# Delta attention: the products of probabilities and values cut into four quarters of TensorE's array

## The reference

```python
def step(carry, seg):
    mem, z = carry
    qq, kk, vv = seg
    sigma_q = jax.nn.elu(qq) + 1.0
    scores = jnp.einsum('bhsk,bhtk->bhst', qq, kk) / scale
    scores = jnp.where(causal_mask, scores, -jnp.inf)
    att_dot = jax.nn.softmax(scores, axis=-1) @ vv
    att_mem = sigma_q @ mem / (sigma_q @ z)
    sigma_k = jax.nn.elu(kk) + 1.0
    delta = vv - sigma_k @ mem / (sigma_k @ z)
    mem_new = mem + jnp.einsum('bhsk,bhsv->bhkv', sigma_k, delta)
    z_new = z + sigma_k.sum(axis=-2, keepdims=True).transpose(0, 1, 3, 2)
    att = beta * att_mem + (1.0 - beta) * att_dot
    out = att.reshape(Bsz, SEG, H * DV) @ Wo
    return (mem_new, z_new), out
```

## Time and profile before

| | us |
|---|---|
| median of 3 runs | 681.11 (678.39 to 682.96) |
| the profiled execution's own time | 681.31 |
| its span in the trace | 679.3 |
| attention, first scores to the last stage's end | about 37 to 425 |

### The profile page before, as it was taken

The page is one execution under the profiler, slowest core; times in us unless marked ns, Lnnn a source line. Parts: engine busy times, 40 slices in busy tenths (PEclk is TensorE's granted clock), DMA queues, the critical chain, the costliest instruction groups (busy, mean ns, idle before and its releaser), DMA issues. The chain is left out here.

```text
span 679.3 us, 12696 instructions
## 1 busy us (share of the span) xinstructions
PE 620.1 (91%) x4390; PEld 523.8 (77%) x4390; DVE 407.5 (60%) x1057; ACT 375.2 (55%) x882; POOL 172.2 (25%) x189
## 2 busy tenths in 40 slices
PE   3999999999999999999999998697999958996796
PEld 3878888988988988988988988586455546985553
DVE  6757595196396196396196273768445479535554
ACT  2679769479569479569469464222466521201242
POOL 4702011011011011011011021342477514301454
PEclk9999999999999999999999999899999978998799
DMA  8200200000120000100000051298233261008631
GB/s 265 78 2 1 81 14 1 3 6 2 34 68 1 2 6 1 32 6 0 5 5 1 3 123 40 73 408 314 62 95 101 73 238 69 0 1 307 235 91 35
DMA packets 25459, 48.99 MB, mean 72 GB/s; under 512 B 4062, under 2 KB 15296, under 8 KB 25408
## 3 DMA queue, kind: packets, MB, share of 16 engines
q1 hardware_dynamic: 19456, 35.74, 15.2%
q0 software_dynamic: 3840, 10.49, 5.1%
q10 hardware_dynamic: 2112, 2.10, 0.9%
HBM read 40.06 MB, written 8.78 MB: 72 GB/s over the span
## 5 line engine op out<-in xcount | busy, mean ns | idle before, releaser
L932 DVE RECIPROCAL denominators<-readings 128x2 f32<-128x2 f32 x128 | 21.3, 167 | 143.8 <-PE readings L572 143.4
L572 PEld LDWEIGHTS readings<-memory_copy,sigma 128*128 128x128 f32 x512 | 75.3, 191 | 11.7 <-ACT memory_copy L779 2.6
L788 ACT ACTIVATE memory_reading<-readings,denominators 64x128 f32<-64x128 f32 x256 | 78.5, 356 | 5.3 <-DVE denominators L932 3.3
L572 PE MATMUL readings<-memory_copy,sigma 128*128 128x129 f32 x512 | 78.7, 275 | 2.6 <-ACT memory_copy L779 2.5
L779 ACT ACTIVATE memory_copy<-memory 128x258 f32<-128x258 f32 x128 | 50.1, 392 | 55.4 <-PE memory L582 40.9
L938 DVE SCALAR_TENSOR_TENSOR minus_delta<-readings,denominators,v 64x128 f32<-64x128 f32 x240 | 73.8, 347 | 4.5 <-DVE denominators L932 0.3
L582 PE MATMUL memory<-minus_delta,sigma_k_tokens 128*128 128x129 f32 x480 | 73.2, 275 | 0.0
L481 POOL TENSOR_TENSOR xn<-scores,exp_sum_inverse 64x512 f32<-64x512 f32 x32 | 33.8, 1055 | 133.8 <-DVE exp_sum_inverse L959 132.6
L472 POOL TENSOR_TENSOR scores<-scores,score_max 128x512 f32<-128x512 f32 x16 | 16.7, 1044 | 195.3 <-DVE score_max L953 195.3
L621 PE MATMUL ahead<-wo,attT 128*128 128x256 f32 x256 | 64.5, 396 | 1.0 <-DVE attT L967 1.0
L582 PEld LDWEIGHTS memory<-minus_delta,sigma_k_tokens 128*128 128x128 f32 x480 | 63.0, 191 | 0.0
(11 more groups left out here) (303 smaller groups left out, 1465.1 us busy)
## 6 DMA issues: line engine op xcount, KB each, us to landing
weights_e<-experts SPq DMA_DIRECT2D x24, 608.0 KB, 12.5
xn<-L_attn_Wq SPq DMA_DIRECT2D x4, 512.0 KB, 4.0
wo<-L_attn_Wo SPq DMA_DIRECT2D x1, 2048.0 KB, 12.9
rows_e<-xn ACTq DMA_DIRECT2D x4, 512.0 KB, 10.8
carried<-L_attn_Wk SPq DMA_DIRECT2D x3, 512.0 KB, 4.8
xn<-L_attn_Wv SPq DMA_DIRECT2D x3, 512.0 KB, 4.0
x<-L_attn_x SPq DMA_DIRECT2D x4, 256.0 KB, 3.5
x<-L_attn_x SPq DMA_DIRECT2D x2, 512.0 KB, 3.5
```

Source lines behind the costliest of these rows:

```text
L572: last = pe.matmul(KQ[g][:, hh * MC:(hh + 1) * MC], sqk[:, GROUP * g + hh, pair, 2 * par:2 * par + 2, :], mz[g][:, hh, :], start=True, sto ...
L788: last = act.activation(read[rows, half, GROUP * g + hh, pair, :], KQ[g][rows, hh * MC:hh * MC + DK], ACT.Copy, scale=nr[g][rows, hh:hh + 1])
```

## The change

Each local product is cut into four matmuls of 64 keys, 64 columns and 64 queries, so that the zero blocks of the probabilities are not multiplied. The two segments of a tile take the two row halves of the array (`par`), and the two halves of a head's 128 columns the two column halves (`c`). A row half writes its own bank, `L[par]`, which now holds both heads. So one burst has 32 matmuls in place of 8, and ScalarE picks each head out of two banks with two instructions of 256 columns. The burst has one semaphore step where it had two. Its waits for `pTs` stand ahead of a full-size matmul: in slot 10 of `project` 10, in slot 14 of `project_out`, and the burst itself comes behind these; where a slot has neither, a transpose of the identity is put in for it (`busy`). Waits for ScalarE's scaling (`bt_copied`) become waits for both heads.

```diff
-                def local(n, half, pp, hh):
-
-                    h = GROUP * pp + hh
-                    pe.wait_ge(pTs_ready, 4 * n + h + 1)
-                    for t in range(TPH):
-                        last = pe.matmul(L[hh][:, t * P:(t + 1) * P], v[:, half * TPH + t, h * DK:(h + 1) * DK],
-                                         pTs[hh][:, t * P:(t + 1) * P], start=True, stop=True)
+                def local(n, half, pp):
+
+                    for hh in range(GROUP):
+                        for t in range(TPH):
+                            for par in range(2):
+                                keys = slice(par * SEG, (par + 1) * SEG)
+                                queries = pTs[hh][keys, t * P + par * SEG:t * P + (par + 1) * SEG]
+                                at = (hh * TPH + t) * SEG
+                                for c in range(2):
+                                    begin = (GROUP * pp + hh) * DK + c * SEG
+                                    last = pe.matmul(L[par][c * SEG:(c + 1) * SEG, at:at + SEG],
+                                                     v[keys, half * TPH + t, begin:begin + SEG], queries,
+                                                     start=True, stop=True)
                     last.then_inc(bt_ready, 1)
...
                     if m == 0:
                         if behind:
-                            pe.wait_ge(bt_copied, 4 * n - 1)
+                            pe.wait_ge(bt_copied, 4 * n)
                         scores(n, half, 0)
...
                     if m == 12:
                         pe.wait_ge(p_ready, 4 * n + 4)
+                        pe.wait_ge(bt_copied, 4 * n + 2)
                         for hh in range(2):
-                            pe.wait_ge(bt_copied, 4 * n + hh + 1)
                             turn_probs(n, 1, hh)
-                    if m in (10, 14):
-                        for hh in range(2):
-                            local(n, half, (m - 10) // 4, hh)
+                    out_at = OUT_AT if ahead else LAST_OUT_AT
+                    if m in (10, 14) and not (ahead if m == 10 else behind and m in out_at):
+                        pe.wait_ge(pTs_ready, 4 * n + (m - 6) // 2)
+                        busy(pe, L[0], ident, 1)
                     if ahead:
                         for what, u in AHEAD_AT.get(m, ()):
+                            if m == 10 and what == "project":
+                                pe.wait_ge(pTs_ready, 4 * n + 2)
                             if what == "turn":
                                 turn_sigma_k(n + 1, 1 - half, u)
                                 continue
...
                             project(n + 1, it + half, 1 - half, u, free)
-                    out_at = OUT_AT if ahead else LAST_OUT_AT
+                    if m == 10:
+                        local(n, half, 0)
+                    if m == 14 and behind and m in out_at:
+                        pe.wait_ge(pTs_ready, 4 * n + 4)
                     if behind and m in out_at:
...
                         project_out(1 - half, out_at[m])
+                    if m == 14:
+                        local(n, half, 1)
...
                 def scale_local(n, half, pp):
 
+                    act.wait_ge(bt_ready, 2 * n + pp + 1)
                     for hh in range(2):
                         h = GROUP * pp + hh
-                        act.wait_ge(bt_ready, 4 * n + h + 1)
-                        act.activation(att[:, half, h, :], L[hh][:, :], ACT.Copy, scale=one_less_q[:, h:h + 1])\
-                           .then_inc(bt_copied, 1)
+                        by_parity = att[:, half, h, :].rearrange("p (t a c) -> p t a c", a=2, c=SEG)
+                        for par in range(2):
+                            src = L[par][:, hh * TPH * SEG:(hh + 1) * TPH * SEG].rearrange("p (t c) -> p t c", c=SEG)
+                            last = act.activation(by_parity[:, :, par, :], src, ACT.Copy, scale=one_less_q[:, h:h + 1])
+                        last.then_inc(bt_copied, 1)
```

More of the change, by code:

```diff
@@ L425, in _ @@
                 next_tiles.load_first(sp, carried)
-                sp.wait_ge(bt_ready, 4 * STAGES)
+                sp.wait_ge(bt_ready, 2 * STAGES)
                 sp.dma_start(x[:, TPH:NT, :], x_tiles[:, TPH:NT, :]).then_inc(x_reloaded[1], 16)
```

## The result

The changed kernel takes 688.85 us (median of 4 runs, 687.24 to 690.48) beside 680.11 for the kernel before in the same job: a ratio of 1.012, interval 1.009 to 1.0149, slower by 6.1 to 10.1 us. Timed again later, it took 687.75 (7 runs) beside 679.98: 1.0093, interval 1.0061 to 1.0125. The median of 688.85 lies inside the stated range of 675 to 693, but above the forecast of 682.0 and past the likeliest case's own 679 to 688; 687.75 lies at that case's edge. With 1.2% and 0.9% the loss is at the limit of 1% that the prediction drew; slower by more than that had 0.23.

The account below looks back on a forecast made before the run. TensorE was taken to bound the attention. Slots 10 and 12 add 4.4 us, slot 14 saves 3.5, the last stage 0.1: +0.8 on the profiled 681.31 gives 682.1, as median 682.0; range 675 to 693.

Parts of the forecast that it names:

- the likeliest case: The prediction's own forecast, a step of four quarter records taking 53 to 88 ns: 679 to 688 us, chance 0.70.
- Part 1: The local burst: four quarters run side by side, 64 records in 1.19 us against 1.78, saving 0.59.
- (b): Rival: record starts are limited to about 25 ns whatever array part they use, 1.82 us a burst; 692 us, chance 0.11.
- (c): Rival: quarters in one row half exclude each other, so each burst takes 2.22 us; 698.5 us, chance 0.09.
- (d): Rival: the new form skips no work, 64 records at the old pace; same as (c), no chance of its own.
- Part 2: Slot 10, seven stages: TensorE stands 1.35 us, not 0.36, for ScalarE's sigma copy; next reading 0.415 us later.
- The term of 0.415: Slot 10: microseconds by which the next reading comes later in each of seven stages, despite the shorter burst.
- Part 3: Scaling and slot 12: ScalarE's four scalings take 1.54 us, so TensorE waits 0.22 us before the transposes.
- The term of 0.22: Slot 12: microseconds TensorE waits for ScalarE's scaling before the transposes, in each of seven stages.
- the later wait in slot 0 costs nothing: Slot 15's scaling ends at 232.71, before the next scores at 233.83, so their wait adds 0.
- The layers behind the attention only shift: After the attention: the later layers move in time only; no change in their length was counted.
- (a): Rival: ScalarE is early enough in slot 10, seven bursts there save 1.06 us each; 670 us, chance 0.07.

Follow-up runs that it names:

- Scaling by bank: Changed kernel with ScalarE's four scalings ordered by bank, not by head, and slot 12 and the next scores waiting for their own bank alone: 684.57 us, ratio 1.0061.
- the version with copies first: Changed kernel with slot 10's burst put back first, scalings ordered by bank, and ScalarE's probability copies ahead of its exponential at slot 9: 675.62 us, ratio 0.9916.
- the exchange on ScalarE: Kernel before, nothing split, with ScalarE's copies of probabilities ahead of the exponential at slot 9: 677.33 us, ratio 0.9958.

## Why the prediction was right or wrong, point by point

- **Part 1, the burst.** Right. 64 records of 218 ns in 1.16 us start every (1160 - 218) / 63 = 15 ns, a step of four every 60, where 63 was taken. What was missed is the 0.1 us by which the first reading behind it is longer. The two projection calls and the burst of slot 14 take 2.17 us (229.34 to 231.51) where they took 2.76: 0.59 saved, as forecast, and 0.49 with the longer reading.
- **The rivals (b), (c) and (d), and the two rules beside them.** All fell. A start every 15 ns is under the floor of about 25 ns that the Trainium skill has in "TensorE: Matmul & The Clock Gate", section "Wait — 56ns, not 53.3ns?". The two quarters of a row half run beside each other, against the rule on row groups in section "The mechanism" of its Part 3. Here the measurement decides.
- **Part 2, slot 10.** The mechanism was right: counted as in the prediction, TensorE is free at 214.22 + 4 x 0.112 = 214.67 and goes on at 216.09, 1.42 us where 1.35 stood, since TensorE goes on 0.14 behind the copy's end (215.95) and not 0.055. The term of 0.415 measured 0.51: 0.47 to the next reading (5.01 for 4.54) and 0.04 in slot 11, where the longer first reading shows. The full-size products in the new place show that it is the order's price: with the burst back ahead, it is gone.
- **Part 3, slot 12.** The four scalings took 1.54 us, as worked out. The term of 0.22 measured 0.42 by the slot's length (the row's 0.22 of idle counts from the end of the update's last record and not from where TensorE could have gone on): ScalarE follows the update behind the burst, which was 0.58 late and not 0.415, and the transposes start 0.14 behind the scaling's end (222.75 to 222.89), not 0.055. The Trainium skill, "TensorEngine Tiling (Array Packing)", section "PSUM Bottleneck", warns that tiling speeds up TensorE and not the copies out of PSUM; this wait, 0.42 us in seven stages, is of that kind, though another order of the same four copies removes it.
- **The step that failed outright: "the later wait in slot 0 costs nothing".** It was read off a stage with an output projection in slot 15. The first stage has none, so its last scaling ends at 81.59, 0.7 us after TensorE is done with the update before, and 0.8 us are lost before the scores of the second stage (the rows on L593 above). Scaling by bank took that back too.
- **"The layers behind the attention only shift".** Wrong by the 1.6 us of the read-back, seen in both profiles. Inside the attention 0.2 to 0.6 us are added once, where the loop jumps back; the 0.4 that the last stage gains up to its last reading about cancels that.
- **The sum.** Seven times 0.51 and 0.42 less six times 0.49 is 3.6; with 0.8 before the scores of the second stage 4.4, the attention's loss. Another 0.3 is the last stage's longer scaling (L619 waits 0.92 us for it, before 0.62) and 1.6 the read-back: 6.3 of a measured 6.1 to 10.1, in the second timing 4.1 to 8.5. The rest, 2.4 and 1.5 us by the two medians, wasn't found in one place. That it is all chance is unlikely: the median less the attention's distance is 298.1 to 299.0 us in all runs without the split, and 299.8 to 302.6 in all eight with it. A lower clock doesn't explain it either, since in the second timing the changed kernel and the kernel before were both granted 0.971 of it on average. What brings it stays open.
- **The forecast.** It added +0.8 us where 8.7 and 7.8 were measured: 4.4 for slots 10 and 12 became 6.5, -3.5 for slot 14 became -2.9, and 0.8, 1.6 and the unexplained rest stood at nothing. The mechanisms of slots 10, 12 and 14 were right; the two waits came out larger and the gain smaller. That the median lies in the range is luck: it reached up to 693 to take in (b), whose mechanism fell. Two of its figures are off by their own terms, and nothing rests on them: the upper end of the wait in slot 12 comes to about 0.5 and not 0.6, the median to 681.9 and not 682.0.
- **The rival (a).** Its condition, ScalarE early enough in slot 10, could be made in part: the version with copies first is at 675.6 and not 670. Of the 1.06 us that (a) has for slot 10, 0.5 came, and as much comes there without the split.

## What to carry to other kernels

Work that an engine does slowly may be what covers another engine's copy: before it is moved or shortened, look for the wait that stands behind it, and ask in which order the other engine does its copies. When a fix comes with another change, run it in the old kernel as well: here the exchange on ScalarE brought in slot 10 as much without the split. A change of tiling changes which results share a bank, so the order in which a bank is emptied has to follow the order in which it is wanted again. A term that is read off one middle stage is to be read off the first and the last as well.

## What the runs showed that was not expected

- Four quarters of the array, 64 rows by 64 columns, run beside each other at one record every 15 ns, and the first full-size reading behind them is 0.1 us longer.
- 14 more loads of instructions come with 48 more records (and as many weight loads) in each burst, 8 of them from 233 to 330 us alone, where the kernel before has none; a loop's body can outgrow what is kept of it between passes.
- A read-back of 512 KB took 5.4 us with a load of instructions 2.7 us behind its issue, 4.1 with one 0.6 us behind, and 3.8 with none near.
- By its median, every version with the split takes at least 0.8 us longer outside the attention than any without it, also where its read-back lands in 3.9 us; the cause is open.
